# Source scores of a chunk as one matmul of 24 columns, its three bf16 parts added by VectorE

## The reference

```python
def _L0(x1, x2, v, adj):          # per head
    scores = q . k * SCALE ; scores = where(adj > 0, scores, NEG_FILL)
    out = softmax(scores) @ v
def _L1(x, adj, W_w, W_b, a):     # per head
    h = (x @ W_w.T + W_b).reshape(N, H, D)
    s_src = einsum('bhd,d->bh', h, a[:D]);  s_dst = einsum('bhd,d->bh', h, a[D:])
    e = leaky_relu(s_src[:, None, :] + s_dst[None, :, :], 0.2)
    attn = softmax(where(adj == 0, -1e9, e), axis=1)
    out = elu(einsum('ijh,jhd->ihd', attn, h))
x = layernorm(x + _L0(x, x2, v, adj))
x = layernorm(x + _L1(x, adj, W_w, W_b, a))
```

## Time and profile before

| | us |
|---|---|
| median of 3 runs | 421.07 |
| lowest and highest | 420.63, 424.67 |
| span of the profiled execution | 421.6 |
| VectorE busy in it | 299.4 |
| TensorE busy | 244.7 |
| GpSimd busy | 216.7 |
| ScalarE busy | 166.0 |

### The profile page before, as it was taken

The page is one execution under the profiler, slowest core; times in us unless marked ns, Lnnn a source line. Parts: engine busy times, 40 slices in busy tenths (PEclk is TensorE's granted clock), DMA queues, the critical chain, the costliest instruction groups (busy, mean ns, idle before and its releaser), DMA issues.

```text
span 421.6 us, 5435 instructions
## 1 busy us (share of the span) xinstructions
PE 244.7 (58%) x1394; PEld 172.8 (41%) x1394; DVE 299.4 (71%) x833; ACT 166.0 (39%) x473; POOL 216.7 (51%) x327
## 2 busy tenths in 40 slices
PE   0572654924596697887688779123582171295690
PEld 0362432613265465564465456012361160173460
DVE  2995989999999999989797849503350351567773
ACT  5312665242462664564335352000100250545546
POOL 7237754370857868617757221771777176073200
PEclk9995575776588689789799995555857575586786
DMA  8875747752867675304523200440444144142201
GB/s 301 329 196 156 250 145 243 266 148 93 317 235 229 230 261 154 102 26 117 153 66 89 89 29 29 108 117 18 114 108 109 36 131 106 50 108 79 79 25 56
DMA packets 24515, 57.93 MB, mean 137 GB/s; under 512 B 6592, under 2 KB 14912, under 8 KB 22432
## 3 DMA queue, kind: packets, MB, share of 16 engines
q0 software_dynamic: 10032, 31.77, 26.8%
q1 hardware_dynamic: 14448, 25.77, 17.3%
HBM read 53.20 MB, written 4.33 MB: 136 GB/s over the span
## 4 chain that ended last, share of the span: by engine, by line
DVE 17%; issue 14%; PE 13%; another core or an unknown queue 9%; ACT 3%; POOL 3%; DVEq 0%; ACTq 0%; POOLq 0%
PE e_po L1446 6%; DVE e_weighted L1720 3%; DVE e_left L1720 2%; PE e_pj L1469 2%; DVE e_y L1492 2%; POOL e_ring L1072 1%; DVE e_run L1691 1%; DVE e_raw L1522 1%; DVE e_prod L1651 1%; DVE e_rden L1490 1%; DVE e_run L1693 1%; DVE e_y L1743 1%; DVE e_y L1483 1%; POOL e_rstd L1096 1%
## 5 line engine op out<-in xcount | busy, mean ns | idle before, releaser
L1072 POOL DMA_INDIRECT e_ring<-in_kv,e_col_i x78 | 80.3, 1029 | 69.6 <-DVE e_col_i L1624 27.0
L1072 POOL DMA_INDIRECT e_ring<-table,e_col_i x78 | 74.2, 952 | 58.5 <-issue 23.2
L1446 PE MATMUL e_po<-e_weighted,e_sel_edges 128*128 128x264 f32 x158 | 50.1, 460 | 10.2 <-DVE e_weighted L1720 7.2
L1427 PE MATMUL e_po<-e_mean_row,e_diagonal 128*128 128x264 f32 x64 | 24.9, 476 | 41.2 <-DVE e_y L1492 25.9
L1446 PEld LDWEIGHTS e_po<-e_weighted,e_sel_edges 128*128 128x128 f32 x158 | 33.3, 226 | 20.5 <-DVE e_weighted L1720 10.2
L1522 DVE MAX8 e_raw<-e_search 128x8 bf16<-128x512 bf16 (+2 forms) x56 | 38.7, 725 | 0.8
L1165 ACT ACTIVATE e_search<-e_search 128x2048 bf16<-128x2048 int32 x16 | 30.5, 1907 | 20.1 <-DVE e_raw L1522 12.1
L1490 DVE RECIPROCAL e_rden<-e_po 128x8 f32<-128x8 f32 x32 | 6.5, 204 | 44.3 <-remote 29.7
L1392 PE MATMUL e_pq<-e_left,e_sel_rows 128*128 128x256 bf16 x156 | 34.2, 317 | 0.0
L1427 PEld LDWEIGHTS e_po<-e_mean_row,e_diagonal 128*128 128x128 f32 x64 | 12.2, 220 | 45.7 <-issue 44.8
L1720 DVE TENSOR_TENSOR e_weighted<-e_ring,e_pc 128x528 f32<-128x528 f32 (+1 forms) x42 | 27.4, 679 | 2.4 <-PE e_pc L1420 2.2
(11 more groups left out here) (221 smaller groups left out, 601.0 us busy)
## 6 DMA issues: line engine op xcount, KB each, us to landing
e_search<-in_adj SPq DMA_DIRECT2D x16, 1024.0 KB
table<-e_hx SPq DMA_DIRECT2D x16, 136.0 KB
e_ring<-in_kv SPq DMA_DIRECT2D x1, 2112.0 KB, 13.4
out<-e_prod SPq DMA_DIRECT2D x16, 128.0 KB
e_ring<-in_kv,e_col_i POOLq DMA_INDIRECT x78
e_ring<-table,e_col_i POOLq DMA_INDIRECT x78
e_xres<-in_x SPq DMA_DIRECT2D x2, 512.0 KB, 5.9
e_xres<-in_x SPq DMA_DIRECT2D x3, 256.0 KB, 6.7
```

What stands on the lines that cost most here:

```text
L1072: nc.gpsimd.indirect_dma_start(out=rings[layer][:, q % RING[layer], :], out_offset=None, in_=kv if layer == 0 else table, in_offset=bass.I ...
L1427: nc.tensor.matmul(po[n % 2][:, 0:CV], diagonal[:, n % 3, :], mean_row[:], start=True, stop=False)
L1446: last = nc.tensor.matmul(po[n % 2][:, 0:CV], selection(layer, q, 1)[:, 0, :], weighted[plan.weighed_into(b)][:, j * CV:(j + 1) * CV], sta ...
```

## The change

The three bf16 parts of a chunk's source scores become one matmul of 24 columns, part beside part, in place of three of 8 columns that PSUM adds up. A group then takes up to 384 columns of pt. The copy on ScalarE, copy_src, is replaced by add_src on VectorE: one tensor_reduce from PSUM that adds the three parts and writes src. The planner gets new times for both, and add_src a rank (-50) that puts it ahead of all other work of VectorE as soon as its input is there. Since the bank is now emptied by two engines, two semaphores count the emptying, turns_copied (ScalarE) and src_added (VectorE), and the stages that use pt wait for both. turn_src raises src_turned in place of edges_turned.

```diff
--- before.py
+++ after.py
@@ -346,7 +346,7 @@
                     ("turn", 0, g - 2) if g >= 2 else None)
             scores = o.last["score"]
         else:
-            put("DVE", 0.65, early, ("score", 1, g), ("copy_src", g), ("gather", 1, (plan.q0[g] + plan.C[g] - 1) | 1), ("turn",) + divmod(n - 2, NG))
+            put("DVE", 0.65, early, ("score", 1, g), ("add_src", g), ("gather", 1, (plan.q0[g] + plan.C[g] - 1) | 1), ("turn",) + divmod(n - 2, NG))
             scores = ("score", 1, g)
         for q, m in plan.quads[g] if layer == 0 else []:
             put("PE", 0.1 * m + 0.15, rank + 0.5, ("turn_edges", q, m), ("move", g), holds="pt")
@@ -413,8 +413,8 @@
     for k in range(NK):
         tile_stages(0, k, plan.group_of_k(k))
     for g in range(NG):
-        put("PE", 0.09 * plan.C[g] + 0.1, g + 2, ("turn_src", g), ("spread", g), holds="pt")
-        put("ACT", 0.3, g + 2, ("copy_src", g), ("turn_src", g), frees="pt")
+        put("PE", 0.035 * plan.C[g] + 0.15, g + 2, ("turn_src", g), ("spread", g), holds="pt")
+        put("DVE", 0.025 * plan.C[g] + 0.1, -50, ("add_src", g), ("turn_src", g), frees="pt")
     put("DVE", 0.25, 90, ("column_sums",), ("copy_norm", NK - 1))
     put("PE", 1.4, 90, ("mean_h",), ("column_sums",), ("evac", NK - 1))
     put("ACT", 0.45, 90, ("copy_mean", 1), ("mean_h",), ("fill", 0, NK - 1))
@@ -907,12 +907,19 @@
         table_stored = [sem(f"e_table_stored{i}") for i in range(2)]
 
         stages = all_stages(plan)
-        turns_before = {}
-        u = 0
+        turns_before, src_turns_before = {}, {}
+        u = u_src = 0
         for stage in stages:
-            if stage[0] in ("turn_edges", "turn_pens", "turn_norm", "turn_src"):
-                turns_before[stage] = u
+            if stage[0] in ("turn_edges", "turn_pens", "turn_norm"):
+                turns_before[stage], src_turns_before[stage] = u, u_src
                 u += 1
+            elif stage[0] == "turn_src":
+                turns_before[stage], src_turns_before[stage] = u, u_src
+                u_src += 1
+
+        def turn_bank_free(eng, stage):
+            at_least(eng, "turns_copied", turns_before[stage])
+            at_least(eng, "src_added", src_turns_before[stage])
 
         def edges_turned(q):
             return [turns_before[st] for st in turns_before if st[0] == "turn_edges" and st[1] <= q < st[1] + st[2]][0]
@@ -1209,11 +1216,6 @@
                     if q + m > TURNED:
                         act.wait_ge(s("sums_done"), plan.reports_by(plan.batch_of[0, q + m - 1 - TURNED]))
                     nc.scalar.copy(selection(0, q, m).rearrange("p c r -> p (c r)"), pt[:, 0:m * P]).then_inc(s("turns_copied"), 1)
-                elif stage[0] == "copy_src":
-                    g = stage[1]
-                    _, _, q0, C_g = lens(g)
-                    act.wait_ge(s("edges_turned"), turns_before["turn_src", g] + 1)
-                    nc.scalar.copy(src[:, q0:q0 + C_g, :].rearrange("p c h -> p (c h)"), pt[:, 0:C_g * H]).then_inc(s("turns_copied"), 1)
                 elif stage[0] == "copy_w":
                     act.wait_ge(s("w_summed"), 1)
                     for k in range(2):
@@ -1334,7 +1336,7 @@
                     CH, X = plan.C[g] * H, REACH[g]
                     pe.wait_ge(s("const_ready"), N_CONST)
                     pe.wait_ge(s("flags_ready"), g + 1)
-                    at_least(pe, "turns_copied", turns_before[stage])
+                    turn_bank_free(pe, stage)
                     at = 0
                     for which in plan.pen_turns[g][i]:
                         some = flags[:, g % 2, which, :]
@@ -1395,12 +1397,11 @@
                     g = stage[1]
                     _, k0, q0, C_g = lens(g)
                     pe.wait_ge(s("src_parts_ready"), g + 1)
-                    at_least(pe, "turns_copied", turns_before[stage])
+                    turn_bank_free(pe, stage)
                     for c in range(C_g):
                         k = k0 + plan.tile_in_group(g, c)
-                        for part in range(3):
-                            last = nc.tensor.matmul(pt[:, c * H:(c + 1) * H], sel(q0 + c), upper(src_parts[:, part, k:k + 1, :])[:, 0, :], start=(part == 0), stop=(part == 2))
-                    last.then_inc(s("edges_turned"), 1)
+                        last = nc.tensor.matmul(pt[:, c * 3 * H:(c + 1) * 3 * H], sel(q0 + c), upper(src_parts[:, :, k, :]), start=True, stop=True)
+                    last.then_inc(s("src_turned"), 1)
                 elif stage[0] == "turn":
                     _, layer, g = stage
                     n = layer * NG + g
@@ -1666,7 +1667,7 @@
                     else:
                         for c in range(0, C_g):
                             arrived(dve, 1, q0 + c)
-                        dve.wait_ge(s("turns_copied"), turns_before["turn_src", g] + 1)
+                        dve.wait_ge(s("src_added"), src_turns_before["turn_src", g] + 1)
                         c = 0
                         while c < C_g:
                             at = (q0 + c) % RING[1]
@@ -1695,6 +1696,11 @@
                     at_least(dve, "exp_ready", n)
                     v.tensor_tensor(shifted[0:CH, :], turned[0:CH, P:2 * P], run[0:CH, X:X + P], ALU.subtract).then_inc(s("shifted_ready"), 1)
                     dve.wait_ge(s("shifted_ready"), n + 1)
+                elif stage[0] == "add_src":
+                    g = stage[1]
+                    _, _, q0, C_g = lens(g)
+                    dve.wait_ge(s("src_turned"), src_turns_before["turn_src", g] + 1)
+                    v.tensor_reduce(src[:, q0:q0 + C_g, :], pt[:, 0:C_g * 3 * H].rearrange("p (c i h) -> p c h i", i=3, h=H), AX_X, ALU.add).then_inc(s("src_added"), 1)
                 elif stage[0] == "choose":
                     q = stage[1]
                     if q == 0:
```

## The result

Twenty executions of each kernel, side by side: the changed one has a median of 422.62 us (413.41 to 426.43), the one before 421.6 (419.15 to 424.67). The ratio is 0.9902, 95% interval 0.9875 to 0.993. The changed kernel's times fall into two groups at the same granted clock, 8 from 413.4 to 419.4 and 12 from 422.0 to 426.4, and the ratio compares the lower group alone with all runs of the kernel before. By that group the change gives 1.0%; over all runs it gives nothing. The profiled execution took 417.35 us (span 415.7), of the lower group; the prediction was 416.1.

What follows compares the result with a forecast made beforehand. VectorE was taken to bound layer 0 and GpSimd's gathers layer 1. From 421.1 us, 5.5 for the shortened pause came off and 0.5 for layer 0 was added: 416.1 us, own range 411 to 419, with rivals 409 to 430.

Steps and rivals of the forecast that it cites:

- rival 1: Late TensorE answers stay as they are, with chooses standing before score in VectorE's queue: 422.4 us, chance 0.28.
- The bound: Whole kernel: VectorE paces layer 0, GpSimd's 78 gathers pace layer 1, one start every 1.25 us, with pauses between.
- TensorE: Seven turn_src stages: 0.027 us a matmul of 24 columns, so 7.4 us becomes 3.15, the saving mostly beside waits.
- VectorE: Seven new reductions on VectorE at 0.15 us plus 1.04 ns an element, 3.0 us in all.
- Layer 0: Reductions falling where VectorE paces layer 0 cost +0.5 us, bounds 0 and 0.9.
- Gathers beside chooses: Layer 1 gathers beside VectorE's chooses take slightly longer: 0.5 us, against 5.2 us by the skill's rule in full.
- TensorE's clock: Less TensorE work near 250 us could bring the clock's fall forward, costing 2 us; a case inside the range.
- The chain and the pause: Source-score chain ends by 267 to 272.5, gate opens near 278.3, pause before gather 18 falls 8.94 to 0.30: 8.6 us.
- The step that failed: Source-score chain in layer 1: TensorE's answers assumed on time, with bursts a third as long and another engine waiting.
- What arrives: End of layer 1: engines, not gathers, hold some 4.4 us, so 5.5 of the 8.6 us arrive.
- Rival 2: A late answer at add_src holds 37 chooses, 7.8 us, on VectorE before score: 429.4 us, chance 0.22.
- Rival 3: The change gives no time, since the new order puts something else on this path: 421 us, chance 0.10.

Runs made afterwards that it cites:

- e7: The changed kernel, unaltered, beside the kernel before, on a second chip without late answers: 386.03 us median of 12 beside 386.95, ratio 0.9987.
- e12: The changed kernel, unaltered, beside the kernel before, on a third chip without late answers: 387.58 us median of 12 beside 387.02, ratio 1.001.
- e2: The changed kernel's instructions in the order of stages of the kernel before: 421.34 us median of 12 beside 424.44, ratio 0.9941.
- e1: The instructions of the kernel before in the changed kernel's order of stages: 430.48 us median of 12 beside 424.44 for the kernel before.
- e6: The changed kernel with 24 filler matmuls behind every reporting batch of sums in layer 1: 397.55 us median of 4, ratio to the kernel before 1.0274.
- e11: The changed kernel with layer 1 gathers allowed to be 26 chunks ahead, not 10: 387.14 us median of 10, ratio to the kernel before 1.0013.
- e8: The kernel before, its planner told that turn_src is cheap and ScalarE's copies go first: 389.04 us median of 10, ratio 1.0061.
- e5: The kernel before, each layer 1 gather indirect but reading one fixed list of 128 consecutive rows: 385.25 us median of 8, ratio 0.9967.
- e4: The kernel before, layer 1's 78 gathers replaced by plain copies of 128 consecutive rows issued by GpSimd: 371.49 us beside 424.44, ratio 0.876.
- e9: The kernel before, layer 1's indirect gathers reading one fixed list of 128 consecutive rows, measured again: 385.39 us median of 8, ratio 0.9961.
- e10: The kernel before, unaltered, profiled on a chip without late answers: 385.97 us median of 8.

## Why the prediction was right, and where not

The time was near for the profiled execution (416.1 for 417.35), and that is in part luck. The prediction had one time where the kernel has two; the median of all 20 executions, 422.62, is beside the 422.4 of rival 1 and above the 416.9 from which the prediction called it faster. For the profiled execution the steps of the forecast can be checked one by one.

**The bound.** VectorE in layer 0, gathers in layer 1: right. On the chips without lateness it is simpler still, 78 gathers on end.

**TensorE.** 0.027 us a matmul, taken from matmuls of 8 and 27 columns: right. Seven stages of 0.37, 0.58, 0.52, 0.56, 0.38, 0.49 and 0.32 make 3.22 us; 3.15 were predicted.

**VectorE.** 0.15 + 1.04 ns an element: right. 0.36, 0.56, 0.46, 0.55, 0.38, 0.42 and 0.29 make 3.02 us for a predicted 3.0.

**Layer 0.** +0.5 predicted, the first gather starts 0.8 later. It can't be told from nothing: the unchanged e7 and e12 start theirs at 261.40 and 264.94.

**Gathers beside chooses.** The first six take 1.06, 0.95, 0.95, 1.02, 0.95 and 1.04, 0.3 us above 0.95 in all: the row's side of what was weighed, not the 5.2 us that the prediction worked out from the rule in the Trainium skill (SBUF — State Buffer, "Who interferes with whom").

**TensorE's clock.** The small case in the range didn't come. The windows of after, as in the earlier trace rows, have the same levels of 1.00 and 0.50:

```profile
240.00:250.00 10.00, 7.92 (x39) 5.14 (x38) 5.68 (x15) 5.29 (x21) 1.54 (x6) 1.00 0.09 30
262.00:284.00 22.00, 8.23 (x27) 5.14 (x26) 13.13 (x53) 0.70 (x2) 16.27 (x17) 0.50 0.38 100
```

VectorE now works 13.1 of the 22 us for 7.5, mostly since score, scan and weigh of group 0 (from 276.26, some 4.3 us) run in what was a wait; reductions and bad_sum make up most of the rest.

**The chain and the pause.** Chain over by 267 to 272.5: it was 265.93. Score of group 0 at 274.4: it was 276.26. Gate open by 278.3: "back" was over at 279.82. Gather 18 with 0.30 before it: right.

**The step that failed** is the reason given for the prompt answers: "Suppose that the chain is answered on time, now that each burst is a third as long and another engine waits." e2 has both and is answered 6.3 and 5.4 us late. What keeps the chain clear is the step that was put at nothing, "all orders after the first turn_src may differ by a place or two". They differ by far more: group 2 moves from 259 to 185 us and group 3 from 263 to 250, ahead of the first indirect gather of layer 1. e1 has only this and has no such pause. The order leaves little of the chain to be late, not nothing: group 6's matmuls and those of bad_sum still ran beside the first gathers (263.19 and 264.44) and were visible at once, where in the trace of before the matmuls that were over by 264.25 were answered 15.7 us late. Why these were not is open, and that too was luck. The order could have been worked out from the planner's entries: the copy's rank falls from g + 2 to -50, and the engine changes. A planner's inputs are part of the change and can be played through like its instructions.

**What arrives.** 5.5 of 8.6 us were predicted to arrive, because the end was held by engines: the last gather is 5.2 us earlier and the span 5.9 shorter. The amount was right, the reason only in part. The shortfall arose before the last gather: the first one starts 0.8 later and the later pauses grew by 2.0 and 0.7.

**The rivals.** Rival 1, lateness stays: true after the sums, but it no longer meets this chain in the profiled run. Rival 2, a late answer at add_src with work queued behind it: not in the profiled run; in e2 it happens twice, with the chooses done by then, and costs about half of the pause. 12 of 20 runs lie at 422 to 426; that in them one more late answer falls on the path is argued from the traces, not shown. Rival 3, nothing gained from a new order: not in the profiled run, but over all 20 executions nothing was gained, and 386.03 against 386.95 and 387.58 against 387.02 say that nothing is gained where nothing is late.

**What the prediction had no case for** is the largest finding. It weighed the lateness as something that the kernel has wherever it runs. It is there on one chip and absent on two others, with the same instructions: 421 to 424 us against 386 to 387. The predicted 1% is a gain on a cost that two of the three chips of the experiments don't have.

**Open.** Why TensorE's completions are held back on one chip beside indirect gathers; whether scatter, filler work (e6) or a looser gate (e11) changes it there; whether e8 would remove the pause without VectorE. e5, e6, e8 and e11 ran on the other chips only. The chip of e1 to e4 was not met again, so a trait of that chip is not told apart from something that went on there at that time. Which chip the first comparison ran on is not recorded; by its level (421.6) and by its two traces, with completions up to 2.6 us late in layer 0 and 14.4 in layer 1, it was one of the same kind.

## What to carry to other kernels

When an engine waits for "remote" or "issue" long after the matmul it needs is over, don't cost the change from that wait as if it were the kernel's own: run the unchanged kernel on another chip first. Work that must cross engines can be put ahead of the stretch where answers are late, but count all executions, not the best group: here that gave 1.0% in 8 of 20 and nothing over all, while shorter stages inside that stretch gave 0.6% over all twelve. And play a planner's new ranks through before calling its order unchanged: the order was the change here.

## What the runs showed of the hardware

- On one chip TensorE's completions became visible up to 16 us after the matmuls ended, several at once, while GpSimd issued the indirect gathers of layer 1. In layer 0, where it issues as many of them, none was over 2.7 us late in the six traces at that level (before, after, e1 to e4); why not is open. With plain copies from GpSimd or SyncE in layer 1, on the same chip, none there was over 0.01 us. On two other chips, with all 78 indirect gathers, none was over 0.01 us late in either layer, in eight traces. The same kernel takes 424.44 us on the one and 386.95 and 387.02 on the others, 9% apart.
- An indirect gather of 128 rows costs GpSimd 0.95 us whether its rows are scattered or consecutive (e9: 959 ns mean, e10: 957), a plain copy of as many rows 0.55.
- A matmul of 24 columns with its own weight load adds 0.027 us to a run of them (16 take 0.56), as one of 8 columns does: three bf16 parts side by side have the price of one.
